# A two-way branch in TensorE's block loop: the general path placed behind the loop body's code, one bank address a block instead of two

## The chip, the cores and the metric

The kernel runs on one core of a Trainium2 chip. The time is the device time of one execution in microseconds; before the change it is 1201.61 us, the median of three runs (1199.98 to 1201.78).

## The reference

One layer of a graph network on 6250 nodes of 128 features and 100000 edges, sorted by destination:

```
h = relu(concat(x[src], x[dst]) @ Wm1 + bm1)
h = relu(h @ Wm2 + bm2)
messages = h @ Wm3 + bm3
agg = segment_sum(messages, dst) / max(count, 1)
upd = relu(concat(x, agg) @ Wn1 + bn1) @ Wn2 + bn2
out = layernorm(x + (x + upd))
```

Hidden width is 256. All of it is float32.

## The kernel before

**Head.** `x @ Wm1` is split into a part for the source node (`a_table`) and one for the destination node (`b_table`), both worked out once per node and stored in DRAM. Weights and activations are split into a high and a low part, so that the fast matmul form gives float32 accuracy with three products.

**Edges.** The sorted edges are cut into 391 blocks of 256. A body handles 4 blocks (U = 4); the bodies 0 and 1 and the last one are unrolled, the others are one hardware loop of 95 passes. In each block k, TensorE (PE) does, in this order in `body`:

- 4 transposes of the gathered rows `a_edge` into a PSUM bank (L1413), behind a wait for `s_ot`, which DVE raises when it has made the block's one-hot matrix;
- 2 matmuls, `expand` (L1324), that add the rows of `b_table` of the block's first 128-row window, picked by the one-hot matrix;
- 4 matmuls that sum the second layer's result of block k-6 into the bank of sums: `first_sum` (L1341) and `other_sums` (L1345, L1347, L1349);
- 12 matmuls of the second layer for block k-2 (L1437).

Each matmul is a weight load (PEld) and a matmul (PE), so a block has 44 instructions for the array. SP loads `b_win` and `rel`, POOL gathers `a_edge` with two indirect DMAs a block (L630), ACT makes the relu and the high parts, DVE the low parts (L1106, L1118) and the one-hot matrices (L1023, L1038).

**Sums by ranges.** Nodes are summed in ranges of 128 rows that begin at multiples of 96. Two halves of `sums` take turns; the registers `own` and `other` hold which half is in use. When a range ends, `begin_range` (L1373 and the lines before) waits for DVE's last addition (`s_add`), swaps the registers and starts the new half, and DVE adds the old half to `agg` with two operations (L1060).

**The word.** For each block a word, worked out at run time from the destinations, tells PE what the block needs: 0 for nothing, bits for windows beyond the first ("far" nodes), for further ranges, and for the end of a range. The words of a body are loaded at its start (L422), behind the loop's branch (L394). In the loop, `with pe.If(word > 0)` (L1418) leads to the general path `expand_and_sum`, which tests each of the bits again (L1381, L1391, L1364, L1394), and `with pe.If(word < 1)` (L1420) leads to the straight path, which has the same matmuls without tests. In the code of each block the general path stands between the transposes and the straight path: a block with word 0 jumps over it at L1418 and falls through L1420, another one falls through L1418 and jumps over the straight path at L1420. `bank_at` (L1337) turns `own` into an address with a register instruction each time it is called, twice in a block. The last jump of an If body, to the instruction right behind it, does not appear in the trace.

**Tail.** 19 matmuls that keep PE busy (L1447), then the node update in groups of 4 windows.

What the change touches is `body` of `@block.tensor` and what it calls.

Of the kernel before, what the change touches and what calls it, by code (L numbers as in the profile page):

```python
# [18 lines left out]
U = 4  # L19
R = 4  # L20
RB = 4
RC = 2
AHEAD = 2
BACK = 6
# [10 lines left out]
def gnn_layer(nc, x, src, dst, Wm1, bm1, Wm2, bm2, Wm3, bm3, Wn1, bn1, Wn2, bn2, out):  # L35
# [25 lines left out]
    with ExitStack() as ctx:  # L61
        def sb(name, shape, dt):
            return ctx.enter_context(nc.sbuf_tensor(name, shape, dt))

        def sem(name):
            return ctx.enter_context(nc.semaphore(name))
# [34 lines left out]
        b_win = sb("b_win", [P, RB, H], F32R)  # L101
        b_far = sb("b_far", [P, H], F32R)
        onehot_t = sb("onehot_t", [P, 3, EB], F32R)
# [162 lines left out]
        s_ex = sem("s_expanded")  # L266
# [12 lines left out]
        s_sg = sem("s_last_segments_summed")  # L279
# [111 lines left out]
        def bodies(e, body):  # L391
            body(0)
            body(1)
            with nc.Fori(2, NI - 1, engines=bass.OrderedEngineSet([e.engine]), head_slot={e.engine: 0}) as i:  # L394
                body(i)
            body(NI - 1)

        def there(i, k):
            return not isinstance(i, int) or 0 <= U * i + k < NBE

        def among_last(i, k, n):

            return isinstance(i, int) and U * i + k >= NBE - n
# [5 lines left out]
        def steps(i, back=BACK):  # L409

            return range(U + back) if isinstance(i, int) and i == NI - 1 else range(U)

        def words_of(i, back=BACK):

            return -(-len(steps(i, back)) // U) * U
# [5 lines left out]
        def load_words(e, words, first, n, top):  # L421
            return nc.values_load_multi_w_load_instructions(  # L422
                words[0:1, bass.ds(first, n)], engines=[e.engine], min_val=0, max_val=top,
                skip_runtime_bounds_check_because=WHY)[1]
# [777 lines left out]
        def _(pe):  # L1202
# [35 lines left out]
            for g in range(NG + 1):  # L1238
# [8 lines left out]
                n, k = size(g), g % 2  # L1247
                if n:
# [3 lines left out]
                    for j in range(n):  # L1252
                        ins = pe.transpose(bank[k][:, j * P:(j + 1) * P], f_x[:, g * GW + j, :], ident[:, :])
# [11 lines left out]
                n, k = size(g - 1), g - 1  # L1265
# [14 lines left out]
                if g == NG:  # L1280
                    pe.wait_ge(s_w3, 48)
                    for c in range(KH):
                        ins = pe.transpose(bank[0][:, c * P:(c + 1) * P], w3[:, c, :], ident[:, :])
# [21 lines left out]
            own = pe.alloc_register("own_bank_pe")  # L1305
# [3 lines left out]
            ended = pe.alloc_register("sums_added_pe")  # L1309
# [12 lines left out]
            def expand(rows, hot, k):  # L1322
                for h in range(KH):
                    ins = pe.matmul(bank[k % 2][:, h * EB:(h + 1) * EB], rows[:, h * P:(h + 1) * P], hot,  # L1324
                                    start=False, stop=True, skip_group_check=True)
                return ins
# [8 lines left out]
            def bank_at(which):  # L1335

                return sums[:, bass.ds(within(pe.snap(which), 0, 512), 512)]  # L1337

            def first_sum(to, slot, k, start):

                return pe.matmul(to[:, 0:HC], onehot[:, slot, 0, :], h2_hi[:, k % U, 0, :], start=start,  # L1341
                                 stop=False, skip_group_check=True)

            def other_sums(to, slot, k):
                pe.matmul(to[:, 0:H], onehot[:, slot, 0, :], h2_lo[:, k % U, 0, :], start=False, stop=False,  # L1345
                          skip_group_check=True)
                pe.matmul(to[:, 0:HC], onehot[:, slot, 1, :], h2_hi[:, k % U, 1, :], start=False, stop=False,  # L1347
                          skip_group_check=True)
                return pe.matmul(to[:, 0:H], onehot[:, slot, 1, :], h2_lo[:, k % U, 1, :], start=False, stop=True,  # L1349
                                 skip_group_check=True)  # L1350
# [27 lines left out]
            def expand_and_sum(i, k, word):  # L1378
                if there(i, k):
                    spans = word & 127  # L1380
                    with pe.If(spans > 0):  # L1381
                        with pe.Fori(1, within(spans, 1, NFE) + 1):
                            expand_far(k)
                    expand(b_win[:, k % RB, :], onehot_t[:, k % 2, :], k).then_inc(s_ex, 1)
                if there(i, k - BACK):
                    if isinstance(i, int) and U * i + k == BACK:
                        pe.wait_ge(s_sz, 1)
                    if not there(i, k):
                        pe.wait_ge(s_h2l[(k - BACK) % U], nth(i, k - BACK))
                    if there(i, k - BACK - 1):  # L1390
                        with pe.If(word > 2**13 - 1):  # L1391
                            sum_all_further(k - BACK - 1, word)
                            begin_range(k - BACK)
                        with pe.If(word < 2**13):  # L1394
                            first_sum(bank_at(own), (k - BACK) % U, k - BACK, False)
                    else:
                        first_sum(bank_at(own), (k - BACK) % U, k - BACK, False)
                    ins = other_sums(bank_at(own), (k - BACK) % U, k - BACK)
                    if among_last(i, k - BACK, BACK + 1):
                        ins.then_inc(s_sg, 1)  # L1400
                elif there(i, k - BACK - 1):
                    sum_all_further(k - BACK - 1, word)

            def body(i):
                words = load_words(pe, words_pe, i * U, words_of(i, BACK + 1), PE_TOP)
                for k in steps(i, BACK + 1):
                    word = words[k]
                    if there(i, k):

                        pe.wait_ge(s_ot[k % U], nth(i, k))  # L1410
                        for t in range(TB):
                            for h in range(KH):
                                ins = pe.matmul(bank[k % 2][:, h * EB + t * P:h * EB + (t + 1) * P],  # L1413
                                                a_edge[:, k % R * TB + t, h * P:(h + 1) * P], ident[:, :],
                                                start=(t == 0 and h == 0), stop=False, is_transpose=True,
                                                skip_group_check=True)
                    if there(i, k) and there(i, k - BACK - 1):
                        with pe.If(word > 0):  # L1418
                            expand_and_sum(i, k, word)
                        with pe.If(word < 1):  # L1420
                            expand(b_win[:, k % RB, :], onehot_t[:, k % 2, :], k).then_inc(s_ex, 1)
                            first_sum(bank_at(own), (k - BACK) % U, k - BACK, False)
                            ins = other_sums(bank_at(own), (k - BACK) % U, k - BACK)
                            if among_last(i, k - BACK, BACK + 1):
                                ins.then_inc(s_sg, 1)
                    else:
                        expand_and_sum(i, k, word)
                    if there(i, k - AHEAD):
                        j = (k - AHEAD) % U
                        if not there(i, k):  # L1430
                            pe.wait_ge(s_h1l[j], nth(i, k - AHEAD))
                            pe.wait_ge(s_bias, U * i + (k - AHEAD + 1))
                        for t in range(TB):
                            to = bank[H2[j]][:, t * H:(t + 1) * H]
                            for a, b in ((0, 0), (0, 1), (1, 0)):
                                for h in range(KH):
                                    ins = pe.matmul(to, h1[:, j, a, h * EB + t * P:h * EB + (t + 1) * P],  # L1437
                                                    w2[:, b, h, :], start=False, stop=(a == 1 and h == KH - 1),
                                                    skip_group_check=True)
                        if among_last(i, k - AHEAD, LAG):  # L1440
                            ins.then_inc(s_w2, 1)
            bodies(pe, body)

            def keep_busy(to, n):
# [7 lines left out]
            for g in range(NG + 2):  # L1452
                n, k = size(g), g % 2
                if n:
# [3 lines left out]
                    for w in range(n):  # L1458
# [3 lines left out]
                        ins = pe.transpose(by_nodes(bank[F_ROW][0:2, :], g, w), f_mean[:, k, w, H:HC], ident[:, :])  # L1462
# [5 lines left out]
                if n:  # L1468
# [3 lines left out]
                    for h in range(KH):  # L1472
                        to = bank[F_HID[j][h]][:, 0:n]
                        pe.matmul(to, b3_rows[:, h * P:(h + 1) * P], f_row[j][:, 0:n], start=False, stop=False,
                                  skip_group_check=True)
                        for c in range(KH):
                            for n_, (a, feat) in enumerate(((0, f_feat), (1, f_feat), (0, f_feat_lo))):
                                ins = pe.matmul(to, wc[:, a, c, h * P:(h + 1) * P], feat[:, j, c, 0:n], start=False,  # L1478
                                                stop=(c == KH - 1 and n_ == 2), skip_group_check=True)
# [34 lines left out]
```

## Time and profile before

| | |
|---|---|
| median of the runs | 1201.61 us |
| span of the profiled execution | 1416.6 us |
| PE busy | 1249.7 us, 88% |
| PE weight loads busy | 1172.0 us |
| DVE busy | 979.6 us |
| POOL busy | 786.5 us |
| ACT busy | 740.6 us |
| granted TensorE clock, mean | 0.993 |

The span runs from the first to the last instruction of the program. The page gives no other time for the profiled execution; its span is 215 us longer than the median of the runs. A busy time is the union of an engine's instructions; control instructions (branches, registers, waits) are in the trace but not in busy time. Matmuls overlap each other, so the pace of PE is to be read from the starts of its instructions, not from their lengths.

### The profile page before, as it was taken

To read this page: it belongs to the slowest core of one execution; us is meant where nothing else is said; L and a number is where in the kernel's file an instruction comes from. 1 tells how busy PE (TensorE), PEld (TensorE's weight loads), DVE (VectorE), ACT (ScalarE), POOL (GpSimd) and SP (SyncE) were. 2 spreads that over 40 slices of the span, in tenths; PEclk is the share of its full clock that TensorE was granted. 3 is DMA by queue.
4 is the path that set the end of the run, shared out by engine and by line. 5 is a ranking of instruction groups with operands and counts; after the bars stand their busy time and mean duration, and the time that the engine had idled before them with its cause. 6 is when DMAs were issued, how large, how long until landed. Compare 5 with 4: busy or idle time off the path is not lost.

```text
span 1416.6 us, 33766 instructions
## 1 busy us (share of the span) xinstructions
PE 1249.7 (88%) x9614; PEld 1172.0 (83%) x9615; DVE 979.6 (69%) x2072; ACT 740.6 (52%) x1392; POOL 786.5 (56%) x814
## 2 busy tenths in 40 slices
PE   6978888888888888888888889988999989899997
PEld 6868888888888888888888888888888888888886
DVE  6846666766766666766766766767767767777676
ACT  3544555555555555555555555555554555545585
POOL 2166666666666666666666666666666666564000
PEclk9999999999999999999999999999999999999999
DMA  9665555545545555555545555455545454554022
GB/s 308 274 234 156 146 144 151 149 141 151 151 140 150 152 142 147 151 143 147 152 139 150 146 143 151 145 144 152 139 147 151 138 150 144 145 151 142 10 67 86
DMA packets 135605, 211.42 MB, mean 149 GB/s; under 512 B 24247, under 2 KB 102669, under 8 KB 134030
## 3 DMA queue, kind: packets, MB, share of 16 engines
q1 hardware_dynamic: 98030, 108.43, 25.3%
q0 software_dynamic: 37536, 102.55, 25.1%
q8 instruction: 14, 0.23, 0.1%
q14 instruction: 25, 0.20, 0.0%
HBM read 188.09 MB, written 22.80 MB: 149 GB/s over the span
## 4 chain that ended last, share of the span: by engine, by line
PE 80%; issue 12%; DVE 2%; SPq 1%; another core or an unknown queue 1%; DMA 1%; ACT 1%; DVEq 1%; ACTq 0%
PE bank L1437 39%; PE bank L1413 11%; PE bank L1324 6%; PE sums L1345 4%; PE sums L1341 4%; PE sums L1347 3%; PE sums L1349 3%; PE bank L1478 2%; PE sums L1491 1%; PE bank L1234 1%; PE bank L1219 1%; PE bank L1461 1%; PE sums L1219 1%; DMA b_win<-b_table 1%
## 5 line engine op out<-in xcount | busy, mean ns | idle before, releaser
L630 POOL DMA_INDIRECT a_edge<-a_table,src_idx x782 | 767.1, 981 | 457.8 <-remote 268.2
L1437 PE MATMUL bank<-w,h 128*128 128x256 f32 x4692 | 661.4, 283 | 104.9 <-issue 102.1
L1437 PEld LDWEIGHTS bank<-w,h 128*128 128x128 f32 x4692 | 596.5, 188 | 119.7 <-issue 118.7
L1106 DVE SCALAR_TENSOR_TENSOR h<-bank,h 128x512 fp32r<-128x512 f32 x391 | 268.7, 687 | 338.4 <-issue 326.7
L732 ACT ACTIVATE h<-bank 128x512 fp32r<-128x512 f32 x391 | 233.8, 598 | 475.3 <-remote 439.2
L721 ACT COPY bank<-b_bc 128x512 f32<-128x512 f32 x391 | 231.5, 592 | 115.2 <-issue 66.7
L1118 DVE SCALAR_TENSOR_TENSOR h_lo<-bank,h_hi 128x512 fp32r<-128x512 f32 x391 | 266.5, 681 | 0.1
L1413 PE MATMUL bank<-ident,a_edge 128*128 128x128 f32 x1564 | 237.4, 274 | 21.1 <-issue 16.6
L740 ACT ACTIVATE h_hi<-bank 128x512 fp32r<-128x512 f32 x391 | 232.6, 595 | 2.8 <-PE bank L1437 2.8
L1413 PEld LDWEIGHTS bank<-ident,a_edge 128*128 128x128 f32 x1564 | 180.3, 140 | 40.5 <-issue 34.2
L1324 PE MATMUL bank<-onehot_t,b_win 128*128 128x256 f32 x782 | 190.3, 325 | 0.0
L1038 DVE SCALAR_TENSOR_TENSOR onehot<-iota,first_node,dst_col 128x256 fp32r<-128x256 int16 x391 | 186.0, 476 | 0.4 <-PE sums L1349 0.3
L1023 DVE TENSOR_SCALAR onehot_t<-rel,node_half 128x256 fp32r<-128x256 int16 x391 | 154.7, 396 | 22.0 <-DMA rel<-rel_dram 2.9
L1341 PE MATMUL sums<-h_hi,onehot 128*128 128x258 f32 x391 | 115.8, 296 | 15.0 <-issue 12.3
L1324 PEld LDWEIGHTS bank<-onehot_t,b_win 128*128 128x128 f32 x782 | 118.6, 192 | 3.3 <-issue 1.0
L1345 PE MATMUL sums<-h_lo,onehot 128*128 128x256 f32 x391 | 116.3, 298 | 1.0
L1347 PE MATMUL sums<-h_hi,onehot 128*128 128x258 f32 x391 | 110.4, 282 | 0.0
L1349 PE MATMUL sums<-h_lo,onehot 128*128 128x256 f32 x391 | 109.6, 280 | 0.0
L1341 PEld LDWEIGHTS sums<-h_hi,onehot 128*128 128x128 f32 x391 | 73.4, 188 | 25.1 <-issue 24.8
L1345 PEld LDWEIGHTS sums<-h_lo,onehot 128*128 128x128 f32 x391 | 73.7, 189 | 13.0 <-issue 12.6
L1347 PEld LDWEIGHTS sums<-h_hi,onehot 128*128 128x128 f32 x391 | 74.2, 190 | 0.0
L1349 PEld LDWEIGHTS sums<-h_lo,onehot 128*128 128x128 f32 x391 | 73.4, 188 | 0.0
(190 smaller groups left out, 682.7 us busy)
## 6 DMA issues: line engine op xcount, KB each, us to landing
b_win<-b_table SPq DMA_DIRECT2D x391, 128.0 KB
rel<-rel_dram SPq DMA_DIRECT2D x196, 128.0 KB
a_edge<-a_table,src_idx POOLq DMA_INDIRECT x782
a_table<-work SPq DMA_DIRECT2D x12, 512.0 KB, 4.6
b_table<-work SPq DMA_DIRECT2D x5, 1024.0 KB
b_table<-h SPq DMA_DIRECT2D x4, 1024.0 KB
f_x<-in_x SPq DMA_DIRECT2D x12, 256.0 KB, 5.2
b_table<-a_edge SPq DMA_DIRECT2D x3, 1024.0 KB, 5.8
```

The costliest lines, as they stand in the source:

```text
L630: pool.indirect_dma_start(a_edge[:, b % R * TB + t, :], None, a_table, bass.IndirectOffsetOnAxis(ap=src_idx[:, b * TB + t:b * TB + t + 1], ...
L721: act.copy(bank[H2[k % U]][:, :], b2_bc[:, :, :].rearrange("p t h -> p (t h)")).then_inc(s_bias, 1)
L732: act.activation(h1[:, k % U, 0, :], bank[k % 2][:, :], ACT.Relu).then_inc(s_h1h, 1)
L740: act.activation(h2_hi[:, (k - LAG) % U, :, 0:H], bank[H2[(k - LAG) % U]][:, :].rearrange("p (t h) -> p t h", t=TB), ACT.Relu).then_inc(s_ ...
L1106: dve.scalar_tensor_tensor(h1[:, k % U, 1, :], bank[k % 2][:, :], 0.0, h1[:, k % U, 0, :].bitcast(F32), ALU.max, ALU.subtract).then_inc(s_ ...
L1118: dve.scalar_tensor_tensor(h2_lo[:, j, :, :], bank[H2[j]][:, :].rearrange("p (t h) -> p t h", t=TB), 0.0, h2_hi[:, j, :, 0:H].bitcast(F32) ...
L1324: ins = pe.matmul(bank[k % 2][:, h * EB:(h + 1) * EB], rows[:, h * P:(h + 1) * P], hot, start=False, stop=True, skip_group_check=True)
L1341: return pe.matmul(to[:, 0:HC], onehot[:, slot, 0, :], h2_hi[:, k % U, 0, :], start=start, stop=False, skip_group_check=True)
L1345: pe.matmul(to[:, 0:H], onehot[:, slot, 0, :], h2_lo[:, k % U, 0, :], start=False, stop=False, skip_group_check=True)
L1347: pe.matmul(to[:, 0:HC], onehot[:, slot, 1, :], h2_hi[:, k % U, 1, :], start=False, stop=False, skip_group_check=True)
L1413: ins = pe.matmul(bank[k % 2][:, h * EB + t * P:h * EB + (t + 1) * P], a_edge[:, k % R * TB + t, h * P:(h + 1) * P], ident[:, :], start=(t ...
L1437: ins = pe.matmul(to, h1[:, j, a, h * EB + t * P:h * EB + (t + 1) * P], w2[:, b, h, :], start=False, stop=(a == 1 and h == KH - 1), skip_g ...
```

## The change

For blocks that are neither at the beginning nor at the end, the two Ifs become one compare-and-branch with two targets. The straight path follows right behind the branch, so a block with word 0 falls through. The general paths ("apart") of the body's four blocks are placed behind the code of all four; each ends in a jump back to the block's "joined" label. At the end of the body's straight code a jump leads over them to "ended". In the straight path, `bank_at(own)` is called once and its result used for all four sums.

```diff
+            def label(i, k, what):
+
+                return f"pe_body{i if isinstance(i, int) else 'loop'}_block{k}_{what}"
+
             def body(i):
                 words = load_words(pe, words_pe, i * U, words_of(i, BACK + 1), PE_TOP)
+                outer = {}
                 for k in steps(i, BACK + 1):
                     word = words[k]
...
                     if there(i, k) and there(i, k - BACK - 1):
-                        with pe.If(word > 0):
-                            expand_and_sum(i, k, word)
-                        with pe.If(word < 1):
-                            expand(b_win[:, k % RB, :], onehot_t[:, k % 2, :], k).then_inc(s_ex, 1)
-                            first_sum(bank_at(own), (k - BACK) % U, k - BACK, False)
-                            ins = other_sums(bank_at(own), (k - BACK) % U, k - BACK)
-                            if among_last(i, k - BACK, BACK + 1):
-                                ins.then_inc(s_sg, 1)
+                        outer[k] = nc.cur_bb
+                        pe.br_cmp(word, 0, on_true=label(i, k, "apart"), on_false=label(i, k, "straight"),
+                                  comp_op="IS_GT")
+                        nc.switch_bb(label(i, k, "straight"), parent=outer[k])
+                        expand(b_win[:, k % RB, :], onehot_t[:, k % 2, :], k).then_inc(s_ex, 1)
+                        to = bank_at(own)
+                        first_sum(to, (k - BACK) % U, k - BACK, False)
+                        ins = other_sums(to, (k - BACK) % U, k - BACK)
+                        if among_last(i, k - BACK, BACK + 1):
+                            ins.then_inc(s_sg, 1)
+                        pe.br(label(i, k, "joined"))
+                        nc.switch_bb(label(i, k, "joined"), parent=outer[k])
                     else:
                         expand_and_sum(i, k, word)
...
+                last = nc.cur_bb
+                pe.br(label(i, 0, "ended"))
+                for k in steps(i, BACK + 1):
+                    if there(i, k) and there(i, k - BACK - 1):
+                        with nc.body(label(i, k, "apart"), parent=outer[k], valid_engines=bass.OrderedEngineSet([pe.engine])):
+                            expand_and_sum(i, k, words[k])
+                            pe.br(label(i, k, "joined"))
+                nc.switch_bb(label(i, 0, "ended"), parent=last)
             bodies(pe, body)
```

## Rows read from the trace of the kernel before

**Rows 1.** The page: its head and busy times.

```profile
span 1416.6 us, 33766 instructions
...
PE 1249.7 (88%) x9614; PEld 1172.0 (83%) x9615; DVE 979.6 (69%) x2072; ACT 740.6 (52%) x1392; POOL 786.5 (56%) x814
```

**Rows 2.** By stage: window, its us, busy us (instructions) of PE, PEld, DVE, ACT, POOL.

```profile
0.00:89.40 89.40, 69.46 (x446) 62.58 (x447) 63.73 (x115) 41.92 (x79) 24.89 (x37) 0.96 0.81 293
89.40:125.00 35.60, 30.07 (x214) 27.93 (x215) 19.10 (x39) 15.99 (x30) 22.23 (x24) 0.90 0.54 156
125.00:1300.00 1175.00, 1044.01 (x8261) 988.30 (x8260) 815.62 (x1622) 610.91 (x1125) 736.38 (x751) 1.00 0.51 147
...
1318.90:1416.60 97.70, 88.59 (x566) 77.14 (x566) 66.19 (x267) 62.13 (x141) 0.00 (x0) 0.97 0.19 59
```

**Rows 3.** Timeline of PE, a block with word 0: start, us, instruction.

```profile
571.60 0.60 PE L1413 MATMUL bank<-ident,a_edge 128*128 128x128 f32 x4
...
572.74 1.58 PE L1437 MATMUL bank<-w,h 128*128 128x256 f32 x12
574.16 0.60 PE L1413 MATMUL bank<-ident,a_edge 128*128 128x128 f32 x4
```

**Rows 4.** Waits of PE's weight loads in the loop: us, times, longest.

```profile
PEld bank L1437 <- issue: 117.8, 190, 1.3
PEld bank L1413 <- issue: 28.9, 49, 1.2
PEld sums L1341 <- issue: 22.7, 46, 0.8
PEld sums L1345 <- issue: 11.9, 57, 0.3
```

**Rows 5.** PE's control by line: ns min/median/max, first and last start.

```profile
L1418 PEldq COMPARE_BRANCH  x384: 68/204/338, 108.2 to 1307.6; - x192
...
L1420 PEldq COMPARE_BRANCH  x384: 72/73/202, 108.6 to 1307.9; - x192
...
L1337 PEldq FUSED_REGOPS  x718: 44/44/44, 106.4 to 1318.2; - x180
...
L1373 PEldq FUSED_REGOPS  x64: 161/166/183, 262.3 to 1316.3; - x64
```

**Rows 6.** The same in short windows: when each stood in time.

```profile
L1418 PEldq COMPARE_BRANCH  x2: 204/204/204, 602.5 to 604.5; - x2
...
L1420 PEldq COMPARE_BRANCH  x2: 73/73/73, 602.7 to 604.7; - x2
...
L1418 PEldq COMPARE_BRANCH  x1: 73/73/73, 608.6 to 608.6; - x1
...
L1418 PEldq COMPARE_BRANCH  x1: 77/77/77, 673.1 to 673.1; - x1
...
L1418 PEldq COMPARE_BRANCH  x1: 338/338/338, 1303.9 to 1303.9; - x1
```

**Rows 7.** Timeline of PE near the loop's end.

```profile
1305.42 0.60 PE L1413 MATMUL bank<-ident,a_edge 128*128 128x128 f32 x4
```

**Rows 8.** Timeline of PE at a range end without lead.

```profile
608.61 0.60 PE L1413 MATMUL bank<-ident,a_edge 128*128 128x128 f32 x4 [0.67 <-issue]
...
610.83 1.35 PE L1437 MATMUL bank<-w,h 128*128 128x256 f32 x10
```

**Rows 9.** Timeline of PE at a range end with a long lead.

```profile
674.07 0.60 PE L1413 MATMUL bank<-ident,a_edge 128*128 128x128 f32 x4
...
675.32 1.34 PE L1437 MATMUL bank<-w,h 128*128 128x256 f32 x10
```

**Rows 10.** DMA queues: packets, MB, share; q8 at 86 to 125, all at 125 to 1300.

```profile
q8 instruction: 4, 0.07, 0.8%
...
q0 software_dynamic: 36019, 98.39, 29.1%
q1 hardware_dynamic: 81113, 73.87, 22.1%
q14 instruction: 6, 0.05, 0.0%
```

## The prediction

> **What bounds the kernel now.** I read the page's head first [rows 1]: the profiled execution spans 1416.6 us, and PE is busy for 88% of it. The page has no other time of that execution, so the span is its own time as far as it can be seen, and what lies around it is not. It is 215 us over the median of the runs, 1201.61 us. That has to be explained before any term can be priced, because the change works on small pauses and the profiled execution has many.
>
> The table by stage [rows 2] splits the span into 89.4 us before the first block of edges, 1229.5 us for the 391 blocks, and 97.7 us of node update. The timeline of an undisturbed block [rows 3] gives PE's own pace: transposes begin at 571.60 and again at 574.16, so a block takes 2.56 us, 22 matmuls one behind the other, the twelve of L1437 about 0.118 us apart (1.42 us from 572.74). So 391 x 2.565 = 1003 us, and 89.4 + 1003 + 97.7 = 1190 us. The runs take 11.6 us more than that, the profiled execution 226 us more. The list of waits in the loop [rows 4] says where most of the 226 are: weight loads of L1437 and L1413 that waited 117.8 + 28.9 us for nothing shown, mostly in the middle of L1437, where there is no branch, register or semaphore, against 22.7 + 11.9 us at L1341 and L1345. The runs have 11.6 us to spare for everything, so they can't hold those pauses; I take them for a cost of being profiled. What is left for the real kernel is PE at its pace, the start (35.6 us for 214 matmuls [rows 2], 9.7 blocks, so some 10.6 us over the pace), and next to nothing else.
>
> **The change part by part.** *Straight block (word 0, 320 of 384).* Before, the sequencer runs four control instructions: the branch of L1418, taken, 204 ns; that of L1420, not taken, 73 ns; two address instructions of L1337, 44 ns each [rows 5]. In the new order the common case falls through, so L1418's becomes 73 ns, L1420's goes, and one of the two of L1337 goes: 131 + 73 + 44 = 248 ns of durations. L1420's starts 0.2 to 0.3 us behind L1418's [rows 6], so each also has some 0.06 us around it; with that it is at most 0.4 us. The jump to "joined" leads to the next instruction and leaves none, as the jumps at the ends of If bodies leave none in the trace; if it did, it takes back at most a taken branch, 0.2 us. On the path all this is worth nothing: what covers it is PE's queue. At the loop's end, where no pause came for two blocks, the branch of a block runs 1.5 us ahead of its transposes (1303.9 against 1305.42 [rows 6, 7]). If that cover were gone, it would be 320 x 0.4 = 128 us, and it would already show as a straight block of over 2.56 us.
>
> *Range end (L1373, 64 times [rows 5]).* Its registers, its three other branches and its wait for s_add stay in their order. The way in turns from a branch not taken (73) into one taken (204): +0.13 us. The way out was L1420's branch, taken there, 202 ns at most, and becomes a jump back: between -0.2 and +0.2 us, I take 0, since both are taken. Whether these count depends on the lead alone. Where the branch stands at 608.6 and the transposes at 608.61, so without lead, the block needs 2.22 us from its transposes to L1437 (610.83) [rows 6, 8]. Where the branch stands at 673.1 and the transposes at 674.07, so with 0.97 us of lead, it needs 1.25 us [rows 6, 9], about as much as a straight block (571.60 to 572.74 is 1.14). So a range end costs about one microsecond less its lead. The 34.6 us before L1341 and L1345 [rows 4] are range ends with little lead, behind a pause of the profiler. Without those pauses the lead is 1.5 us in blocks 1 to 3 of a body and less in block 0, which follows the loop's own branch and the load of the words; the one in [rows 9] is such a block, with 0.97. So only block 0's range ends, some 16 of 64, can lose now, up to 0.1 us each: the change lifts their lead by up to 0.4 and asks 0.13 more, -1.6 to 0 us, and I take the middle.
>
> *Loop edge.* One jump over the general code, new, 95 times: between 0 and 0.2 us each (a taken branch, [rows 5]). It lies on the sequencer, which saved up to four times 0.4 in the same pass: 0 on the path. If the lead were gone, 19 us.
>
> The Trainium skill, "Advanced Engine Details and Errata", section Control Flow Timing, puts an unconditional branch at about 51 ns; by that these jumps cost a quarter of my bound, and the sum stays.
>
> *Code placement.* The number of instructions in a body changes by a handful. The q8 queue fetches code in packets of 16 KB: 4 of them while the first bodies run, and none in the 1175 us of the loop [rows 10], so its code, straight and general path together, stays on chip. A fetch keeps the queue busy for about 0.8% of 16 x 39 us / 4 = 1.25 us. The boundaries move against the code, so one or two fetches at the start or the end can become exposed or hidden: 0, between -2.5 and +2.5 us.
>
> *DVE and POOL* are untouched and stand just behind PE: in the loop 8261 / 22 = 375 blocks, so DVE 815.6 / 375 = 2.17 us a block and POOL 736.4 / 375 = 1.96 [rows 2], without what lies between their instructions. A faster PE sequencer would find little room in front of them either.
>
> **Sum.** Straight 0, range ends -0.8, loop edge 0, placement 0: 1201.6 becomes 1200.8, given as 1201.0. A measurement of this kernel tells about 0.2% (2.4 us) from no change.
>
> **Rivals.** *Faster: the pauses at range ends are in the real runs too.* Then part of the 11.6 us that the runs have over the pace is theirs, and not the start's. For: they are the only pauses tied to this code [rows 4], and the start's 10.6 us were measured in the profiled execution, which inflates them. Against: the spare time is small, and the lead is long wherever no profiler's pause precedes. A range end behind a straight block would gain 0.4 - 0.13 = 0.27 us, 64 x 0.27 = 17, capped by what is there: -3 to -9 us, around 1196. Chance 0.20.
>
> *Slower: the way out to the general path and back is paid at every range end.* Place: L1418's branch, now taken, and the jump back to "joined". Price 0.13 + up to 0.2 us, 64 times: +8 to +21 us, around 1210. It decides where the lead is under one microsecond. For: 46 of the range ends in the profiled loop pause before L1341 [rows 4]. Against: the runs have no room for these pauses. Chance 0.07.
>
> *Slower: leaving the straight code drops the code that was loaded.* A trip out and back would fetch 16 KB: 64 x 1.25 = +80 us, 1280 and more. Against: before, the loop jumps past its general code in every block and fetches nothing [rows 10], and the total length stays. Chance 0.03. A smaller form, fetches more exposed at the start and the end by 3 us, gives 1204.5; chance 0.04.
>
> The Trainium skill, "Runtime: NRT & Kernel Launch", section Instruction fetch mechanics, speaks for this rival: a taken branch whose target lies outside the two pages of code held stalls for a fetch. The trace shows no fetch in the loop so far; by the rule the far jump would bring them.
>
> *The change doesn't do what it says*: the jump to "joined" stays as an instruction in each straight block. The sequencer's saving halves, the time is that of the forecast.
>
> **How the numbers follow.** Forecast 0.66, within 2.4 us. The faster rival 0.20, the three slower ones 0.14. The range takes the forecast's own 1199.2 to 1204.0, the placement's bounds, and most of the faster rival: 1195 to 1206. It leaves out the paid trips (0.10) and the far tail of the faster case (0.05).
>
> **What would show it.** In the profile after: L1418's branch at 73 ns by median, L1420's gone, L1337's count of 718 down by about 320; the timeline of an undisturbed block still 2.56 us; no q8 packet in the loop; the profiler's pauses inside L1437 still there, so that the span may move by tens of microseconds while the runs don't. I am wrong if the runs fall by over 2.4 us (the sequencer was on the path in real runs), or rise with q8 packets in the loop.

## The result, and the profile after

The changed kernel takes 1215.89 us (median of 4 runs, 1213.08 to 1217.35) against 1201.69 before: ratio 1.0114, 95% interval 1.0098 to 1.013. It is 14 us slower. I had forecast no difference (1201.0, range 1195 to 1206), with 0.14 for slower.

The profiled execution of before (1416.6 us) was not like its runs. The kernel `one_bank` below is the one before with a single edit that changes nothing measurable, and its profiled execution spans 1199.3 us. I read that one in the place of before. The table of stages of `one_bank`, then of after, cut at the first transposes, at blocks 8, 14, 388 and 390 (columns: window, its us, busy us and instructions of PE, PEld, DVE, ACT, POOL, granted clock, share and GB/s of the DMA engines):

```profile
0.00:88.39 88.39, 69.01 (x446) 62.07 (x447) 63.43 (x115) 41.95 (x79) 24.88 (x37) 0.96 0.83 297
88.39:107.94 19.55, 17.24 (x129) 16.14 (x129) 12.36 (x24) 10.84 (x20) 14.78 (x16) 0.91 0.67 194
107.94:124.67 16.73, 15.88 (x132) 15.59 (x133) 12.26 (x25) 9.53 (x19) 12.65 (x14) 1.00 0.64 175
124.67:1086.79 962.12, 962.12 (x8231) 962.12 (x8229) 793.31 (x1618) 615.93 (x1123) 716.62 (x747) 1.00 0.61 178
1086.79:1091.99 5.20, 5.20 (x47) 5.20 (x45) 3.94 (x9) 3.56 (x7) 0.00 (x0) 1.00 0.62 194
1091.99:1199.30 107.31, 98.11 (x638) 85.88 (x636) 74.28 (x283) 65.89 (x148) 0.99 (x2) 0.98 0.17 54
```

```profile
0.00:90.23 90.23, 68.14 (x446) 60.75 (x448) 63.78 (x115) 41.80 (x79) 24.72 (x37) 0.96 0.81 290
90.23:111.23 21.00, 18.09 (x129) 17.60 (x129) 12.85 (x27) 11.02 (x20) 16.06 (x17) 0.84 0.66 196
111.23:128.21 16.98, 16.98 (x133) 16.98 (x134) 11.38 (x23) 9.44 (x18) 11.56 (x13) 0.90 0.54 153
128.21:1095.41 967.20, 967.03 (x8231) 963.73 (x8230) 793.99 (x1618) 611.64 (x1123) 711.66 (x747) 1.00 0.60 178
1095.41:1106.65 11.24, 7.47 (x46) 6.84 (x45) 5.09 (x12) 3.71 (x7) 0.00 (x0) 0.85 0.27 92
1106.65:1213.80 107.15, 97.91 (x638) 85.77 (x636) 73.37 (x282) 65.54 (x147) 0.99 (x2) 0.97 0.16 54
```

Three places hold the 14.5 us between the spans: blocks 14 to 387 take 967.20 instead of 962.12 (+5.1), the two blocks 388 and 389 take 11.24 instead of 5.20 (+6.0), and everything up to block 14 takes 128.21 instead of 124.67 (+3.5). The tail is the same. In `one_bank` PE is busy for all of the 962.12 us, and each of its blocks 14 to 387 takes 2.57 to 2.58 us from transposes to transposes, so this loop runs at PE's pace without a pause.

PE's control instructions after, by line (ns min/median/max, first and last start).
```profile
L1424 PEldq COMPARE_BRANCH  x384: 64/67/4276, 105.6 to 1105.0; - x192
...
L1337 PEldq FUSED_REGOPS  x396: 44/44/44, 104.0 to 1115.4; - x198
...
L1453 PEldq COMPARE_BRANCH  x96: 169/169/288, 106.7 to 1093.3; - x96
...
L1458 PEldq COMPARE_BRANCH  x62: 169/169/176, 237.3 to 1100.7; - x62
...
L394 PEldq COMPARE_BRANCH  x96: 67/209/3364, 107.1 to 1093.6; - x96
```

The change did what it says on the sequencer: the branch falls through in 67 ns where L1418 took 204 [rows 5], L1337 is down from 718 to 396, and no "joined" jump appears in the straight path. What it brought besides is L1453, 96 times 169 ns, and one branch of 4276 ns.

That one is the first instruction of block 388's range end. The timeline of PE after around it, and the granted clock in three stretches (same columns as above):

```profile
1095.41 0.60 PE L1418 MATMUL bank<-ident,a_edge 128*128 128x128 f32 x4
1099.43 0.50 PE L1324 MATMUL bank<-onehot_t,b_win 128*128 128x256 f32 x2 [3.42 <-issue]
1100.27 0.38 PE L1341 MATMUL sums<-h_hi,onehot 128*128 128x258 f32 x1 [0.34 <-issue]
...
1101.21 2.76 PE L1446 MATMUL bank<-w,h 128*128 128x256 f32 x12
1103.77 0.91 PE L1418 MATMUL bank<-ident,a_edge 128*128 128x128 f32 x4
```

```profile
1095.70:1099.20 3.50, 0.31 (x3) 0.07 (x1) 1.31 (x4) 0.21 (x1) 0.00 (x0) 1.00 0.77 272
1099.20:1103.80 4.60, 4.02 (x19) 3.63 (x20) 2.43 (x5) 1.60 (x3) 0.00 (x0) 0.69 0.03 8
1103.80:1108.00 4.20, 4.20 (x35) 4.20 (x34) 2.12 (x4) 2.08 (x4) 0.00 (x0) 0.93 0.00 2
```

PE stands still for 3.42 us behind the transposes. The branch began at 1094.7 us, 0.7 us before them; this head start of the sequencer over the array is called the lead below. The code queue q8 moves two packets between 1095 and 1101 us and none between 128 and 1095:

```profile
q8 instruction: 2, 0.03, 3.1%
```

Behind the stop the granted clock is 0.69, a mix of the two levels of 1.2 and 2.4 GHz, and the twelve matmuls of L1446 take 2.76 us where they take 1.58 elsewhere.

The loop's 5.1 us are at the range ends of block 0 of a body. The timelines of block 188, a block 0 and a range end, in `one_bank` and after:

```profile
572.29 0.60 PE L1413 MATMUL bank<-ident,a_edge 128*128 128x128 f32 x4
...
572.97 0.28 PE L1341 MATMUL sums<-h_hi,onehot 128*128 128x258 f32 x1
573.09 0.28 PE L1345 MATMUL sums<-h_lo,onehot 128*128 128x256 f32 x1
...
573.44 1.58 PE L1438 MATMUL bank<-w,h 128*128 128x256 f32 x12
574.86 0.38 PE L1413 MATMUL bank<-ident,a_edge 128*128 128x128 f32 x2
```

```profile
577.61 0.60 PE L1418 MATMUL bank<-ident,a_edge 128*128 128x128 f32 x4
577.97 0.48 PE L1324 MATMUL bank<-onehot_t,b_win 128*128 128x256 f32 x2
578.28 0.33 PE L1341 MATMUL sums<-h_hi,onehot 128*128 128x258 f32 x1
578.62 0.38 PE L1345 MATMUL sums<-h_lo,onehot 128*128 128x256 f32 x1
578.83 0.28 PE L1347 MATMUL sums<-h_hi,onehot 128*128 128x258 f32 x1
...
580.49 0.38 PE L1418 MATMUL bank<-ident,a_edge 128*128 128x128 f32 x2
```

In `one_bank` the block lasts 2.57 us, after 2.88: the sum at L1345 starts 0.34 us behind the one at L1341, where `one_bank` has 0.12, and everything behind it is late by as much. The list of PE's waits in the loop (us in total, times, longest) has one line after, and none in `one_bank`:

```profile
PEld sums L1345 <- issue: 3.5, 17, 0.2
```

### The profile page after: what moved, and what is told of

It is laid out like the page before. It is cut to its first block, busy times and chain, and to the rows that moved or that the text cites. A ratio compares the mean times of both kernels' runs of the same rounds, so it can differ in the third digit from the quotient of the medians.

```text
span 1213.8 us, 33218 instructions
## 1 busy us (share of the span) xinstructions
PE 1175.6 (97%) x9614; PEld 1151.7 (95%) x9615; DVE 960.4 (79%) x2072; ACT 743.2 (61%) x1392; POOL 765.0 (63%) x814
## 4 chain that ended last, share of the span: by engine, by line
PE 94%; DVE 1%; DMA 1%; SPq 1%; issue 1%; POOL 0%; ACT 0%; DVEq 0%
PE bank L1446 46%; PE bank L1418 14%; PE bank L1324 8%; PE sums L1345 4%; PE sums L1341 4%; PE sums L1347 4%; PE sums L1349 4%; PE bank L1496 3%; PE sums L1509 2%; PE bank L1234 1%; DMA a_table<-work 1%; PE bank L1219 1%; PE bank L1479 1%; PE sums L1219 1%; PE bank L1492 0%
## 5 line engine op out<-in xcount | busy, mean ns | idle before, releaser
L630 POOL DMA_INDIRECT a_edge<-a_table,src_idx x782 | 745.6, 953 | 270.3 <-issue 136.3
L1446 PE MATMUL bank<-w,h 128*128 128x256 f32 x4692 | 621.2, 282 | 0.0
L1446 PEld LDWEIGHTS bank<-w,h 128*128 128x128 f32 x4692 | 584.9, 189 | 0.0
L1418 PE MATMUL bank<-ident,a_edge 128*128 128x128 f32 x1564 | 236.2, 274 | 6.9 <-DVE onehot_t L1023 4.6
L1418 PEld LDWEIGHTS bank<-ident,a_edge 128*128 128x128 f32 x1564 | 181.9, 141 | 7.9 <-DVE onehot_t L1023 5.4
L1023 DVE TENSOR_SCALAR onehot_t<-rel,node_half 128x256 fp32r<-128x256 int16 x391 | 141.7, 363 | 49.9 <-DMA b_win<-b_table 35.6
L1341 PE MATMUL sums<-h_hi,onehot 128*128 128x258 f32 x391 | 111.6, 285 | 0.5 <-issue 0.3
L1345 PE MATMUL sums<-h_lo,onehot 128*128 128x256 f32 x391 | 111.8, 286 | 0.2
L1347 PE MATMUL sums<-h_hi,onehot 128*128 128x258 f32 x391 | 111.2, 284 | 0.0
L1349 PE MATMUL sums<-h_lo,onehot 128*128 128x256 f32 x391 | 110.0, 281 | 0.0
L1345 PEld LDWEIGHTS sums<-h_lo,onehot 128*128 128x128 f32 x391 | 74.0, 189 | 3.9 <-issue 3.9
L1341 PEld LDWEIGHTS sums<-h_hi,onehot 128*128 128x128 f32 x391 | 73.7, 188 | 1.1 <-issue 0.9
```

The lines of the kernel that those rows point to most:

```text
L630: pool.indirect_dma_start(a_edge[:, b % R * TB + t, :], None, a_table, bass.IndirectOffsetOnAxis(ap=src_idx[:, b * TB + t:b * TB + t + 1], ...
```

## The experiments

Theory A says that the three places are three causes: a shorter lead of PE's sequencer in block 0, a fetch of far code at the last body's range end, and a longer entry into the loop. The rivals blame the single bank address, or the far placement as such. The table is worked out from the starts in each kernel's timeline (us): to block 14, blocks 14 to 388, blocks 388 and 389, the longest time of a branch on the word and of the loop's own (L394), and the lead of block 0 in the loop: the median time by which its branch on the word starts before its transposes.

```
kernel               runs     to 14   loop    388-389  word's   L394's  lead 0
one_bank             1202.4   124.7   962.1    5.2     0.34     2.81    1.11
after                1215.9   128.2   967.2   11.2     4.28     3.36    0.85
after_again          1214.6   126.4   967.0   12.1     5.28     3.06    0.85
body1_inline         1213.1   122.7   966.8   13.9     5.96     2.11    0.85
unrolled_apart       1209.7   128.0   962.1   11.1     4.39     2.90    1.11
k0_inline            1212.2   128.6   965.0   11.0     4.54     3.40    0.84
loop_apart           1206.9   123.7   966.9    5.5     0.34     3.49    0.85
last_inline          1206.0   124.3   967.1    5.5     0.34     1.99    0.85
apart_behind_loop    1204.3   124.9   963.4    5.5     0.34     2.19    1.11
near_behind          1203.3   124.9   963.6    5.4     0.21     2.75    1.10
before_8_waits       1208.1   126.1   968.5    5.2     0.43     2.59    1.10
before_slot80        1202.3   126.1   962.1    5.4     0.33     3.17    1.12
one_bank_slot160     1201.7   125.5   962.2    5.2     0.34     0.22    1.12
```

**The bank address alone.**

```diff
-                            first_sum(bank_at(own), (k - BACK) % U, k - BACK, False)
-                            ins = other_sums(bank_at(own), (k - BACK) % U, k - BACK)
+                            to = bank_at(own)
+                            first_sum(to, (k - BACK) % U, k - BACK, False)
+                            ins = other_sums(to, (k - BACK) % U, k - BACK)
```

> The kernel before with one bank address in the straight path, and nothing moved. Theory A (the loss is made of code fetches outside the loop and of a short lead in block 0 of each body): 1201 to 1203 us, no difference from before. Theory B (the moved bank address itself delays the sums): most of the 14 us, 1210 or more. The profile also tells whether the many pauses inside L1437 that the profile of before shows come back with almost the same code.

1202.41 us, ratio 0.9996 (0.9985 to 1.0008). No difference: that part of the change costs nothing and brings nothing. The pauses inside L1437 of the profile of before [rows 4] did not come back, here or in any other kernel, so they belonged to that one execution; I had put them down to being profiled in general. What they came from was not found.

**The change in the loop alone.** Bodies 0, 1 and the last keep the two Ifs.

```diff
-                    if there(i, k) and there(i, k - BACK - 1):
+                    if there(i, k) and there(i, k - BACK - 1) and isinstance(i, int):
+                        with pe.If(word > 0):
+                            expand_and_sum(i, k, word)
+                        with pe.If(word < 1):
...
+                    elif there(i, k) and there(i, k - BACK - 1):
```

> The change in the hardware loop alone; bodies 0, 1 and the last keep their general path inside (with one bank address). Theory A: the 5.8 us stop at block 388 goes, and the longer entry into the loop goes; the 17 range ends in block 0 still pay 0.3 us each: 1206 to 1208. Theory B (far placement as such costs, through the jumps of the loop): 1214 to 1216, as after.

1206.93 us, ratio 1.0043 (1.0026 to 1.006). The loop takes 966.9 us as after, the last body 5.5 as in `one_bank`. The sixteen range ends of block 0 between blocks 14 and 388 last 2.85 to 2.93 us instead of 2.57.

**The change in the unrolled bodies alone.** The same edit with `not isinstance(i, int)`.

> The other half: the change in the unrolled bodies alone, the loop as before. Theory A: the stop at block 388 (about 5.8 us) and the entry into the loop (1.6 us plus what the clock loses behind it) stay, no loss in block 0: 1208 to 1211. Theory B: 1202.

1209.67 us, ratio 1.0067 (1.0049 to 1.0085). The loop is back at 962.1, the stop at block 388 is there. The two halves make +4.4 and +7.1 us over the 1202.56 measured beside them: together 11.5 us, where the whole change cost 14.2 in the first comparison and 11.8 in the second (`after_again` below).

**The last body inside again**, the rest as after.

> After, but the last body keeps its general path inside. Theory A (the stop of 5.8 us at block 388 is the fetch of far code): 1209 to 1211, 5 to 6 us under after, with block 388's period near 2.9 us instead of 8.4. Rival (the stop comes from leaving the loop, wherever the general path stands): 1215 to 1216.

1206.04 us, ratio 1.0032 (1.0021 to 1.0042). Its branches on the word never take over 0.34 us, and block 388 lasts 2.90 instead of 8.36 us. In the timeline of PE in `last_inline` it needs 1.48 us from its transposes to L1460, where after needs 5.80 (1095.41 to 1101.21):

```profile
1091.38 0.60 PE L1422 MATMUL bank<-ident,a_edge 128*128 128x128 f32 x4
...
1092.86 1.58 PE L1460 MATMUL bank<-w,h 128*128 128x256 f32 x12
```

So the stop comes from the place of the general path and not from leaving the loop. The median fell by 9.8 us, more than the 5 to 6 expected; the rest is the start (124.3 against 128.2), on which more below.

**Block 0 of the loop inside again**, the rest as after (the two Ifs where `k == 0` and the body is the loop's).

> After, but in the loop's block 0 the general path stands inside again. Theory A: block 0's range ends have their way in for 73 ns instead of 204 and need no jump back, which lifts them over the threshold only in part, as the jump at the body's end stays: the 17 stretches of 0.3 us shrink to 0.1 to 0.2 us: 1212 to 1215. If the place of the code in the loop doesn't matter for them: 1216.

1212.2 us, ratio 1.0076 (1.0058 to 1.0093), and its block 0 range ends last 2.72 to 2.80 us: nearly half of the 0.30 went (the median is 2.74). The rest is not the way in: the lead is 0.84 us, as short as after.

**Each general path right behind its own straight path.** The straight path falls through as after, and jumps over the general path of its block.

```diff
                         pe.br(label(i, k, "joined"))
+                        with nc.body(label(i, k, "apart"), parent=outer[k], ...):
+                            expand_and_sum(i, k, word)
+                            pe.br(label(i, k, "joined"))
                         nc.switch_bb(label(i, k, "joined"), parent=outer[k])
...
-                last = nc.cur_bb
-                pe.br(label(i, 0, "ended"))
```

> The straight path still falls through, but each block's general path stands right behind it, inside the block, and the straight path jumps over it. Theory A: no stop at block 388, a normal entry into the loop; the way into the general path still costs 204 ns instead of 73 but no jump at the body's end is needed, so block 0's lead is near 1.0 us and its range ends lose 0 to 0.2 us: 1202 to 1205. Rival (fall-through as such, with its taken branch into the general path, makes the loss): 1207 or more.

1203.32 us, ratio 1.0009 (0.9997 to 1.0021). The lead in block 0 is 1.10 us, its range ends last 2.63 to 2.68, no stop at block 388. So falling through in the common case costs next to nothing by itself, and brings nothing either.

**The loop's general paths behind the whole loop**, so that a pass ends without a jump.

```diff
             with nc.Fori(2, NI - 1, ...) as i:
-                body(i)
+                more = body(i)
+            if more is not None:
+                more()
             body(NI - 1)
```

Here `more` sets the "ended" jump and the four general paths once, behind the loop's end.

> As loop_apart, but the loop's four general paths stand behind the whole loop, so that no jump is left at the end of a pass. If that jump (169 ns and its 0.1 us) is what shortens block 0's lead from 1.11 to 0.85 us: the lead is 1.1 again, block 0's range ends lose 0.05 to 0.1 us as in near_behind instead of 0.30, and the time is 1202 to 1204, 3 to 4 under loop_apart's 1206.9; one fetch more of 1 to 3 us at the first range end is possible. If the loss comes from the jumps into and out of the far path: 1206 to 1208.

1204.28 us, ratio 1.0011 (1.0002 to 1.0021), loop 963.4. The code is further away than in `loop_apart`, and the loss is a quarter of it: the lead is back at 1.11 us, and block 0's range ends last 2.63 to 2.69. So three quarters of the loss are the jump at the end of a pass, and none is the distance. The quarter that is left is the same as in `near_behind`, where only the way in is longer. The single fetch it adds (one q8 packet at 323 us) shows no stop above 0.1 us in the blocks around it, and no branch on the word takes over 0.34. So far code is not slow by its distance alone.

**A dose of control at range ends**, in the kernel before.

```diff
                             sum_all_further(k - BACK - 1, word)
+                            if not isinstance(i, int):
+                                for _ in range(8):
+                                    pe.wait_ge(s_const, 1)
                             begin_range(k - BACK)
```

> The kernel before, with eight waits on a semaphore that has long been reached (four instructions of the sequencer, some 0.4 us) ahead of the swap of banks at each of the loop's range ends. If the lead hides a range end's control up to about 1.1 us in block 0 and 1.6 us in blocks 1 to 3: only block 0's 16 range ends lose, 0.2 to 0.3 us each: +3 to +5 us, 1205 to 1207. If every range end pays: 61 x 0.4 = +24 us, 1226. If there is no threshold to speak of and all is hidden: 1202.

1208.13 us, ratio 1.0056 (1.0042 to 1.0071), about one over the expected 1205 to 1207. Block 0's range ends last 2.92 to 2.97 us, +0.36 each instead of the expected 0.2 to 0.3; the others stay at 2.57 but for five in block 2, of 2.61 to 2.87. The timeline of PE at block 188, the same place as in the two fences above:

```profile
575.88 0.60 PE L1416 MATMUL bank<-ident,a_edge 128*128 128x128 f32 x4
...
576.56 0.38 PE L1341 MATMUL sums<-h_hi,onehot 128*128 128x258 f32 x1
576.94 0.38 PE L1345 MATMUL sums<-h_lo,onehot 128*128 128x256 f32 x1
...
578.82 0.27 PE L1416 MATMUL bank<-ident,a_edge 128*128 128x128 f32 x1
```

The waits of the 61 range ends in the loop, on the line of the eight and on the next wait (L1372, in `begin_range`):

```profile
L1395 PEldq EVENT_SEMAPHORE  x183: 51/51/51, 234.2 to 1086.6; - x183
...
L1372 PEldq EVENT_SEMAPHORE  x61: 51/51/51, 234.5 to 1086.7; - x61
```

The eight waits became four instructions, three on L1395 and one on L1372. In the trace of block 188 they start 0.106 us apart, and `begin_range`'s register instruction behind them starts 0.42 us later against the transposes than in `one_bank` (0.449 against 0.025 us). They cost nothing in most of the blocks with a lead of 1.63 us. In block 0, where it is 1.10, they cost nearly their whole length: of 0.42 us, 0.36 was lost. A lead of 1.1 us is thus just enough for a range end of the kernel before, with about 0.05 us to spare.

**The loop's head at another slot of its fetch block.** `head_slot` 80, then 160, for PE instead of 0.

> The kernel before, with PE's loop head at slot 80 of a fetch block instead of slot 0, so that the loop is entered within the block of code that body 1 already runs in. If the 2.8 us of the loop's first branch are a wait for the next block of code: the branch takes 0.2 us, and 1198 to 1201 us come out, 2 to 4 under before. If they are something else: 1202, the branch as long as before.

1202.33 us, ratio 1.0001 (0.9989 to 1.0014); the branch still took 3.17 us.

> The kernel before with one bank address and PE's loop head at slot 160 of a fetch block. Slot 80 had changed nothing, which fits a head that still lies in the next block. If at slot 160 the head lies in the block that body 1 ends in: the loop's first branch takes 0.2 to 0.4 us instead of 2.8, and 1198 to 1201 us come out, under before. If not: the branch stays near 3 us and the time at 1202.

1201.71 us, ratio 0.9998 (0.9986 to 1.001). PE's control on the line of the loop, from `one_bank_slot160`:

```profile
L394 PEldq COMPARE_BRANCH  x96: 76/208/218, 106.5 to 1085.7; - x96
```

Now the longest of these branches takes 218 ns, where `one_bank` has 2.81 us and a stop of PE that goes with it. The first stops of PE in the loop's first blocks, in the timeline of `one_bank`, then of `one_bank_slot160`:

```profile
107.94 0.65 PE L1413 MATMUL bank<-ident,a_edge 128*128 128x128 f32 x4 [1.39 <-issue]
...
114.18 0.66 PE L1413 MATMUL bank<-ident,a_edge 128*128 128x128 f32 x4 [0.85 <-DVE onehot_t L1023]
```

```profile
113.16 0.60 ACT L732 ACTIVATE h<-bank 128x512 fp32r<-128x512 f32 x1 [3.23 <-issue]
...
114.13 0.69 DVE L1106 SCALAR_TENSOR_TENSOR h<-bank,h 128x512 fp32r<-128x512 f32 x1 [2.79 <-ACT h L732]
...
115.14 0.55 PE L1413 MATMUL bank<-ident,a_edge 128*128 128x128 f32 x3 [1.36 <-DVE onehot_t L1023]
```

The stop behind the branch is gone with nothing changed but where the loop's code begins, so it was a wait for code. But PE then runs into the next one: it waits 1.36 us for the one-hot matrix of DVE, which waited 2.79 us for ACT, which had stood for 3.23 us for nothing that the profile shows. `one_bank` has the same wait for DVE, only shorter. In both, this block 10 starts 25.8 us behind the first transposes (114.18 less 88.39, 115.14 less 89.33): the stop of 1.39 us cost `one_bank` nothing. The expected 1198 to 1201 was missed. ACT's stop lies at its own entry into the loop. Its control instructions of the loop's line, from `one_bank_slot160`, columns as above:

```profile
L394 ACTq FUSED_REGOPS  x95: 44/44/50, 112.7 to 1076.9; - x95
...
L394 ACTq MOVE  x1: 29/29/29, 109.0 to 109.0; - x1
```

The MOVE at 109.0 us stands ahead of the loop, the first register instruction inside it comes at 112.7, and between them a second queue for instructions, q14, moves two packets. That looks like the same wait for code on ACT, but no run moved ACT's loop head, so it is not shown.

**Once more, and with body 1 inside.**

> The changed kernel once more, unchanged, in the same call as the others. If the three places account for the difference (5.1 us at the range ends of block 0, 6.0 at block 388, 1 to 3 at the entry into the loop): 1213 to 1216 us, with the same stretches in its profile.

1214.63 us, ratio 1.0097 (1.008 to 1.0113): loop 967.0, blocks 388 and 389 12.1, the branch 5.28 us.

> After, but body 1, which has one general path only, keeps it inside. If the longer entry into the loop comes from body 1's general path standing between its code and the loop: the loop's first branch is 0.5 to 1.5 us shorter and the time 1 to 2 us less than after_again. If the entry varies by itself: same as after_again.

1213.06 us, ratio 1.0094 (1.0075 to 1.0113). The entry branch is 0.95 us shorter than in `after_again` and the time 1.6 us less, as expected if body 1's general path were the cause, but `last_inline`, whose body 1 is that of after, has 1.99. The interval covers the ratio of `after_again`. So whether body 1's placement matters was not settled; the time to block 14 goes from 122.7 to 128.6 us over the kernels, and is 128.2 and 126.4 in two executions of the very same one.

## Why the prediction was wrong

**What held.** *Straight block*: saved on the sequencer, worth 0 on the path; block periods stay at 2.57 us. *The bank address*: 0. *DVE and POOL*: not the bound, in any kernel. *A range end costs about one microsecond less its lead*: confirmed by the dose. The lead of 1.5 us in blocks 1 to 3 was close (1.63 measured).

**Loop edge, the step that failed first.** I wrote that the new jump "lies on the sequencer, which saved up to four times 0.4 in the same pass: 0 on the path". Savings do not add up over a pass. In blocks 1 to 3 the lead is 1.63 us before and after, although the sequencer has 0.4 us less to do: it stands at its end and waits. I conclude that a full queue sets it, though no run varied the queue. What counts in block 0 is what comes between block 3 and its own branch, and there the change only added: the lead fell from 1.11 to 0.85 us, by 0.26, the jump's 169 ns and the space around it. `apart_behind_loop` takes the jump away, and the lead is 1.11 again.

**Range ends, wrong in sign.** I had "the change lifts their lead by up to 0.4 and asks 0.13 more". It lowered the lead by 0.26 and asked 0.13 more: 0.39 us against a reserve that the dose of eight waits puts at about 0.05. That leaves 0.34, and 0.30 was measured, sixteen times: 4.8 of the 5.1 us. The rest is one range end in block 2 (block 362, 2.89 us), whose lead was only 0.99. Without the jump, 0.13 less 0.05 leaves 0.08, and `near_behind` and `apart_behind_loop` lose 0.06 to 0.12. My lead of 0.97 for block 0, from [rows 6, 9], was near the real 1.11, and so was the count of sixteen. Reserve and demand were in hand; the sum was made with the wrong sign for the change of the lead.

**The start** (+3.5 us in one execution, +1.8 in the other). In the first, 1.84 us of it lie before the first transposes (90.23 against 88.39), where no line is changed; over the thirteen executions of the table that start spreads from 87.3 to 91.2 us. The rest comes from the entry into the loop. The timeline of PE after there:

```profile
111.23 1.11 PE L1418 MATMUL bank<-ident,a_edge 128*128 128x128 f32 x4 [2.29 <-issue]
...
112.56 0.42 PE L1341 MATMUL sums<-h_hi,onehot 128*128 128x258 f32 x1
...
115.34 0.60 PE L1418 MATMUL bank<-ident,a_edge 128*128 128x128 f32 x4
```

PE stands for 2.29 us where it stood for 1.39 in `one_bank`, and the block behind takes 4.11 us instead of 2.67, its matmuls of L1341 0.42 instead of 0.28: the granted clock is 0.61 between 111 and 115.4 us. `after_again` and `k0_inline` show the same with stops of 1.97 and 2.14, but `loop_apart` has 2.06 and keeps its clock. The +0.9 and +1.4 are partly made good, since PE no longer waits for DVE at block 10. That the entry branch takes 2.0 to 3.5 us is so with and without the change; what sets its length was not found. So of the three places the first two are explained, and the start is open: it differs between executions by as much as it differs between the kernels.

## What to carry to other kernels

Time saved on a sequencer is only worth what its lead lacks: where the lead is capped, look at each place where it is short, and count what comes right before it. A jump at the end of a loop pass falls on exactly such a place. And rarely used code is cheap to move away only if it is held when it is needed: inside the loop the far trips brought no fetch at all, at the last body one trip cost about 6 to 9 us. So leave it inside in the parts that run once. None of the versions here beats the kernel before; `one_bank`, its twin, already runs its loop without a pause.

## What was not expected of the hardware

The lead of PE's sequencer ends at 1.63 to 1.65 us in every kernel in which it was read, some 14 of the matmuls that start 0.118 us apart. PE's branches mostly take 64 to 77 ns when not taken, 202 to 210 taken, 169 unconditional; the one to the last body's far code takes 4.3 to 6.0 us, with packets on q8 at the same time. And a profiled execution can be 18% longer than the runs of the same kernel (1416.6 against 1201.6 us [rows 1]) with a mean granted clock of 0.993.
